# Cross attention: the softmax division of E moves from ACT to GpSimd

## The reference, cut to what matters

```python
q = (x @ Wq + bq).reshape(b, s, 16, 128).transpose(0, 2, 1, 3)
k = (ctx @ Wk + bk).reshape(b, se, 4, 128).transpose(0, 2, 1, 3)
v = (ctx @ Wv + bv).reshape(b, se, 4, 128).transpose(0, 2, 1, 3)
k, v = jnp.repeat(k, 4, axis=1), jnp.repeat(v, 4, axis=1)
q, k = _rmsnorm(q, qn_w), _rmsnorm(k, kn_w)
scores = jnp.einsum('bhsd,bhed->bhse', q, k) / sqrt(128) + attention_mask
probs = jax.nn.softmax(scores, axis=-1)
out = jnp.einsum('bhse,bhed->bhsd', probs, v)
out = out.transpose(0, 2, 1, 3).reshape(b, s, 2048) @ Wo
x = _layernorm(x + out)
```

## Time and profile before

| | |
|---|---|
| time, median of 3 runs | 3014.51 us (3012.94 to 3017.65) |
| the profiled execution's own time | 3019.52 us |
| its span, first to last instruction | 3017.7 us |
| mean granted TensorE clock | 0.949 of full speed |
| busy in the span: PE, PEld | 2734.9 us, 2442.4 us |
| busy in the span: DVE, ACT, POOL | 2017.4 us, 1669.3 us, 1790.0 us |

### The profile page before, as it was taken

How to read it: one execution, slowest core, us unless ns; L and a number is a source line. 1 busy time by engine, 2 the same in 40 slices (tenths; PEclk the granted TensorE clock), 3 DMA queues, 4 the chain that set the end, 5 groups by cost and what they waited for, 6 DMA issues and landing times.

```text
span 3017.7 us, 47826 instructions
## 1 busy us (share of the span) xinstructions
PE 2734.9 (91%) x15794; PEld 2442.4 (81%) x15794; DVE 2017.4 (67%) x3921; ACT 1669.3 (55%) x4244; POOL 1790.0 (59%) x2193
## 2 busy tenths in 40 slices
PE   8699999978999999997699789999999996979998
PEld 7588887857888888875599678888888885869998
DVE  5477777755887888887356456767667676864334
ACT  2265555536888888774455455555655552643222
POOL 0277777734676777665246287888898896630000
PEclk9799999987999999998799899999999998989999
DMA  6635554544433333332411321212212202532101
GB/s 213 197 113 169 155 158 150 155 152 137 129 96 113 114 103 109 108 92 84 140 51 52 127 82 64 93 44 66 78 58 64 74 30 78 178 122 77 33 28 33
DMA packets 209286, 310.76 MB, mean 103 GB/s; under 512 B 47351, under 2 KB 104739, under 8 KB 206931
## 3 DMA queue, kind: packets, MB, share of 16 engines
q1 hardware_dynamic: 209042, 307.70, 32.6%
HBM read 211.27 MB, written 96.37 MB: 102 GB/s over the span
## 4 chain that ended last, share of the span: by engine, by line
PE 49%; POOL 23%; DVE 14%; issue 7%; ACT 4%; DMA 3%; SPq 0%; POOLq 0%; ACTq 0%; DVEq 0%
PE bank L168 9%; PE bank L169 8%; PE bank L170 8%; POOL mh_quant_d L747 6%; PE bank L1621 4%; POOL mh_quant_d L741 3%; POOL mh_quant_d L743 3%; POOL mh_quant_d L745 3%; PE bank L1605 3%; PE bank L1562 3%; POOL me_rl L3171 2%; PE bank L1026 1%; PE bank L1595 1%; PE bank L2091 1%; PE bank L2092 1%
## 5 line engine op out<-in xcount | busy, mean ns | idle before, releaser
L747 POOL TENSOR_TENSOR mh_quant_d<-mh_quant_a,mh_quant_d 128x512 f32<-128x512 f32 x208 | 283.2, 1361 | 17.3
L822 ACT ACTIVATE mh_quant_d<-mh_quant_d 128x512 f32<-128x512 f32 x256 | 161.5, 631 | 229.0 <-POOL mh_quant_d L747 228.6
L725 DVE TENSOR_REDUCE mh_quant_err<-mh_quant_d 128x8 f32<-128x512 f32 x256 | 173.6, 679 | 56.5 <-ACT mh_quant_d L822 54.4
L741 POOL TENSOR_SCALAR mh_quant_d<-mh_quant_a 128x512 f32<-128x512 f32 x208 | 142.0, 683 | 87.2 <-DVE mh_quant_err L725 48.5
L2321 POOL TENSOR_TENSOR fq_var<-fq_mv,eps_ln 100x1 f32<-100x1 f32 x16 | 3.7, 230 | 315.4 <-DVE fq_mv L2264 315.4
L1605 PE MATMUL bank<-ga_eT,ga_v 128*128 128x400 f32 (+1 forms) x384 | 170.9, 527 | 10.6 <-DVE ga_zl L1792 10.6
L1562 PE MATMUL bank<-ga_xt,ga_wqh 128*128 128x400 f32 x512 | 178.4, 411 | 1.6 <-DVE ga_xt L164 1.6
L1756 ACT ACTIVATE ga_e<-ga_e,ga_nm 100x361 f32<-100x361 f32 x256 | 152.7, 596 | 42.5 <-DVE ga_nm L1851 40.4
L780 POOL TENSOR_TENSOR ga_quant_d<-ga_quant_a,ga_quant_near 128x512 f32<-128x512 f32 x128 | 165.3, 1292 | 13.4 <-DVE ga_quant_err L725 2.9
L1752 ACT ACTIVATE ga_e<-ga_e,ga_rs 100x361 f32<-100x361 f32 x256 | 152.5, 596 | 19.2 <-DVE ga_rs L1833 19.2
L1879 POOL TENSOR_TENSOR ga_qrs<-ga_qms,minus_half 100x4 f32<-100x4 f32 x64 | 68.2, 1065 | 158.9 <-DVE ga_qms L1786 158.9
(11 more groups left out here) (435 smaller groups left out, 10356.1 us busy)
## 6 DMA issues: line engine op xcount, KB each, us to landing
keys_turned<-kv_kt SPq DMA_DIRECT2D x16, 1448.0 KB, 6.0
ga_kt<-keys_turned SPq DMA_DIRECT2D x64, 362.0 KB, 3.0
ga_xt<-x_turned SPq DMA_DIRECT2D x48, 400.0 KB, 5.0
mh_xt<-x_turned SPq DMA_DIRECT2D x48, 400.0 KB, 4.7
kv_rows<-qkv SPq DMA_DIRECT2D x50, 320.0 KB, 3.4
qkv<-m_rows SPq DMA_DIRECT2D x16, 960.0 KB
raw<-x SPq DMA_DIRECT2D x64, 200.0 KB
kv_ctx<-in_ctx SPq DMA_DIRECT2D x32, 256.0 KB, 4.7
```

The source lines that it names most:

```text
L725: nc.vector.tensor_reduce(self.of(self.err, i)[:, s, :], self.error(i, s), AX, ALU.add).then_inc(self.summed.sem, 1)
L741: nc.gpsimd.tensor_scalar(e, a[:], 1.0 / SHRINKS[s], MAGIC, ALU.mult, ALU.add).then_inc(made.sem, 1)
L747: nc.gpsimd.tensor_tensor(e, a[:], e, ALU.subtract).then_inc(self.diff.sem, 1)
L822: nc.scalar.activation(self.error(i, s), self.error(i, s), ACT.Square).then_inc(self.squared.sem, 1)
```

## The change

The multiplication of E by the reciprocal of its row sum, E[0:361] of 100 partitions in place, leaves ACT's loop and enters POOL's loop. It keeps the turn (unit n-1 in turn n), what it waits for (`recip`) and what it tells (`scaled`). On ACT it stood behind everything else of the turn and ahead of the exponential; on POOL it stands first in the turn, ahead of `query_rs` and of the quantiser's half trial. Its form changes from an activation with a scale of one value per partition to a `tensor_scalar` with the same value per partition and a second multiplication by 1.0.

```diff
@@ do_act
-                if 1 <= n <= NU:
-                    o = n - 1
-                    since(act, recip, o)
-                    nc.scalar.activation(E[o % 4][:, 0:S2], E[o % 4][:, 0:S2], ACT.Copy, scale=rs[o % 4][:])\
-                        .then_inc(scaled.sem, 1)
                 if n < NU:
                     since(act, maxed, n)
                     nc.scalar.activation(E[n % 4][:, 0:S2], E[n % 4][:, 0:S2], ACT.Exp, bias=nm[n % 4][:],
@@ do_pool
             for n in range(NT):
+                if 1 <= n <= NU:
+                    o = n - 1
+                    since(pool, recip, o)
+                    nc.gpsimd.tensor_scalar(E[o % 4][:, 0:S2], E[o % 4][:, 0:S2], rs[o % 4][:], 1.0, ALU.mult, ALU.mult)\
+                        .then_inc(scaled.sem, 1)
                 if n < NU and sum_at(n) is not None:
                     query_rs(sum_at(n))
```

## The result

The changed kernel takes 3027.13 us (median of 5 runs, 3021.60 to 3030.36) against 3014.51 us before: a ratio of 1.0039, 95% interval 1.0027 to 1.0051, so 11.8 us slower. The forecast of no change, 3012 us, was wrong; the time lies inside the range of 3004 to 3045 us.

What follows compares the result with a forecast made beforehand. It took PE to bound the groups it fills (40.6 us), with DVE setting most of the rest. 3019.5 - 6.7 + 4.0 = 3016.8 us for the profiled execution, 3012 us as median, called no change; range 3004 to 3045 us.

Steps and rivals of the forecast that it cites:

- The relief of ACT: ACT without the division: 3.6 us in ACT's stretches plus half of 6.1 us through POOL, 6.7 us gained, 9.8 at most.
- The price of the division: One division on POOL, 100x361 with one value per partition, taken as a one-input instruction: 0.50 us.
- two-input bound: Upper price if the per-partition value costs like a second tensor: 0.97 us; rival that POOL becomes the bound, 3074 us, chance 0.14.
- POOL's room: POOL's work per group, 31.9 us before and 39.9 us with 16 divisions, said to fit under PE's 40.6 us.
- point for a group that PE fills: Division price at which POOL's room ends in a group of 40.6 us filled by PE: 0.54 us.
- the point of 0.74 us: Division price at which POOL's room ends in the average group of 43.7 us; above it the change was to be slower.
- ACT's square: Square waiting for POOL's subtraction: moved about 0.4 us by one division, 0.49 us given back by ACT, called even.
- POOL's side: Cost of the division on POOL, counted only as more holds of DVE instructions: 4 us, between 0 and some 15.
- a longer wait of the square: Sign of a wrong prediction: ACT's square waits for POOL by much more than now; no size given.
- rival of more holds: DVE held more often in its quantiser steps, 15.6 us more less 6.7 us relief: 3023 us, chance 0.18.
- Holds between DVE and POOL: DVE instructions held while POOL runs: 8.3 us now, growing by 2.1 us plus turn 1's quantiser steps, taken as 4 us.
- PE's transposes: PE's transpose of E, 3.2 us after the reciprocal starts, covers division and POOL's lag, so no wait for the division.

Runs made afterwards that it cites:

- e1: Kernel before with ACT's division taken out and none added on POOL, so E stays undivided: 3001.70 us, ratio 0.9953.
- e14: Kernel before with ACT dividing only the odd units, in the turns that also hold the square; even units stay undivided: 3017.68 us, ratio 0.9996.
- e8: Changed kernel with the division shared: POOL divides odd units in even turns, which have no subtraction, ACT the even units: 3004.71 us, ratio 0.9959.
- e4: Kernel before, division on ACT, plus an extra POOL instruction of the division's shape behind the same wait for the reciprocal: 3037.93 us, ratio 1.0076.
- e2: Changed kernel with ACT's square of the quantiser's difference moved behind the exponential of the same turn: 3014.44 us, ratio 1.0002.
- e6: Changed kernel with POOL's division moved behind the quantiser's half trial of the same turn: 3037.86 us, ratio 1.0064.
- e11: Changed kernel with each POOL division one turn later (unit n-2 in turn n), at its old place in the turn: 3037.20 us, ratio 1.0066.
- e12: Kernel before plus e4's extra POOL instruction and wait in odd turns alone, ahead of the subtraction: 3031.67 us, ratio 1.0041.
- e13: Kernel before plus e4's extra POOL instruction and wait in even turns alone, which have no subtraction: 3015.07 us, ratio 0.9990.
- e7: Changed kernel with the quantiser's clamp on POOL done on one of its eight blocks of 64 columns: 3013.45 us, ratio 0.9984.

## Why the prediction was wrong

**The relief of ACT: mis-sized.** The term was 6.7 us, with 9.8 us as its end; e1 gives 14 us. e14 and e8 show where it lies: in the turns in which ACT also squares.

**The price of the division: somewhat low.** 0.50 us was taken, 0.61 us measured on average, 0.57 us in the median; far from the two-input bound of 0.97 us. (The rows that spoke against the bound were of three kinds, not four.) Twice DVE's time, 1.19 us by the general rule of the Trainium skill (GPSIMD Engine Reference, "Key points"), was not it; the exception for one input in its "Engine selection" was nearer.

**POOL's room: the sum was right and was read too kindly.** With the measured rows a group costs POOL 8 x 3.22 + 4 x 1.07 + 16 x 0.61 + (10.4 + 10.4 + 6.3) / 16 = 41.6 us. The prediction's own point for a group that PE fills was 0.54 us per division; 0.61 us is over it, and that group went from 40.6 to 41.9 us. I had looked at the point of 0.74 us for the average group.

**ACT's square: the step that failed.** The prediction walked one stretch, found that one division moves the subtraction by 0.4 us and that ACT gives 0.49 us back, and called it even. That held POOL to be on time at the start of the stretch. The trace shows that it mostly is not: 0.9 us of idle before `query_rs`, a wait for the reciprocal ahead of only 37 divisions, a lag that goes from turn to turn, and 80.6 us of waits of the square in place of 10.0 us. POOL's side, put at 4 us, costs 0.76%, some 23 us, in e4. The prediction named a longer wait of the square as a sign of being wrong, but no rival and no price stood behind it. Its rival of more holds came to 3023 us, near the measured time; that is luck, since the holds did not grow.

**Holds between DVE and POOL: moved, not grown.** The term was +4 us. L700 fell from a median of 828 to 171 ns and the query weights of L164 from 872 to 686 ns. But L705 rose from 682 to 1345 ns, and the output weights of L164 from 683 to 958 ns on average. L705 before, then the changed kernel's rows (min/median/max ns):

```profile
L705 DVE SCALAR_TENSOR_TENSOR ga_quant_a<-ga_quant_w x8: 681/682/683, 713.7 to 1313.4; 128x512 f32<-128x512 f32 x8
...
L705 DVE SCALAR_TENSOR_TENSOR ga_quant_a<-ga_quant_w x8: 681/1345/1557, 713.6 to 1323.4; 128x512 f32<-128x512 f32 x8
...
L164 DVE TENSOR_TENSOR ga_wql<-raw,ga_wqh x16: 679/686/1124, 675.9 to 1186.2; 128x512 fp32r<-128x512 f32 x16
...
L700 DVE TENSOR_SCALAR ga_quant_base<-ga_quant_base x8: 170/171/400, 711.5 to 1321.0; 128x8 f32<-128x8 f32 x8
```

DVE's busy time over the whole span fell by 5 us. That turn 1 would now find POOL busy (L705) was right; that rival is not the cause, since e2 keeps the long L705 and loses nothing. The prediction let a hold that falls on POOL count for little. But the division on POOL is held too: 611 ns on average against 570 in the median is 10.5 us over 256 of them, and the place at 943 us stands behind two that took 1.27 and 1.01 us, beside weight pieces on DVE (L164). How much of POOL's lag comes from that, no run separates.

**PE's transposes: nearly right.** They wait 7.8 us for the division, where no wait was forecast. The 3.2 us were read at one place; the least is 2.2 us, and e6 and e11 show that the cover was thin.

**Still open.** e12 and e13 together, +0.41% and -0.10%, do not make e4's +0.76%. That the load of the one takes the idle time in which POOL would make up for the other is argued only. It fits e7, and it fits that POOL waits for the reciprocal ahead of 93 of 128 instructions in e12, but of 58 of 256 in e4.

## What to carry to other kernels

Room on an engine is not enough when its queue is in order: list what already hands results to others from there, and ask where the moved work stands ahead of each hand-over and whether the lag is made up before the next. Before moving all of a repeated step, look for the turns in which the new engine has no hand-over and the old one is tightest; half the move in those turns (e8, -0.41%) beat the whole (+0.39%). And a wait at the head of a queue for work that is not urgent, as ACT's square ahead of its exponential, carries every delay of the other engine into the main loop.

## What the runs showed of the hardware

A `tensor_scalar` on POOL of 100x361 with one value per partition took 560 ns at least and 570 ns in the median, against medians of 614 to 622 ns for 128x512 with two immediates: 1.58 against 1.2 ns per column, the fixed part included. It reached 1275 ns at most.

DVE's L700 and L705 are held when they start during a POOL subtraction; the masked scores are not (594 ns in the median in both kernels). Before, L700 started during a subtraction in seven of eight cases and ended 0.02 to 0.03 us behind it (at 965.69 us, the subtraction at 965.67). In the changed kernel it never does, and took 171 ns in the median in place of 828; there L705 starts during a subtraction in seven of eight cases, and ends about 0.55 us behind it.
